# The scatters' stage of a graph layer kernel without TensorE: rows made by VectorE in one step, a predicated copy for crossing rows, no lag between groups

## The reference

```python
x = layernorm(x + L0(x, edge_attr, edge_index))        # attention per destination, 8 heads
# L1:
h = x @ W
e = leaky_relu((h @ a1)[src] + (h @ a2)[dst], 0.2)
attention = softmax(e)                                 # one softmax over all 25000 edges
msgs = attention[:, None] * h[src]
x = layernorm(x + segment_sum(msgs, dst, num_segments=50000))
```

## Time and profile before

| what | value |
|---|---|
| time, median of 3 runs | 1059.08 us (1057.36 to 1061.64) |
| the profiled execution's own time | 1056.71 us |
| its span in the profile | 1055.0 us |
| granted TensorE clock, mean | 0.84 |
| busy over the span: PE, DVE, ACT, POOL | 662.7, 807.1, 705.4, 761.1 us |
| first scatter, last scatter | 790.49, 1046.08 us |
| scatters of this stage | 196 + 1, 195.1 + 1.0 us busy |

### The profile page before, as it was taken

The page is one execution under the profiler, slowest core; times in us unless marked ns, Lnnn a source line. Parts: engine busy times, 40 slices in busy tenths (PEclk is TensorE's granted clock), DMA queues, the critical chain, the costliest instruction groups (busy, mean ns, idle before and its releaser), DMA issues.

```text
span 1055.0 us, 14618 instructions
## 1 busy us (share of the span) xinstructions
PE 662.7 (63%) x3270; PEld 448.6 (43%) x3270; DVE 807.1 (77%) x3723; ACT 705.4 (67%) x2036; POOL 761.1 (72%) x801
## 2 busy tenths in 40 slices
PE   0467777777787677787655656656566555556640
PEld 0246555555565555565444545545432111111110
DVE  4789999999988798896876666666548777777760
ACT  3659998999899797997423444534447666666650
POOL 6777777777777777777077777777737777777775
PEclk9979998999889898988868787878858788778775
DMA  7666786787767678657348777887743322332310
GB/s 200 197 190 200 222 278 210 237 264 231 226 220 238 213 222 258 202 194 226 122 140 285 254 255 248 277 271 248 222 132 93 96 85 86 88 94 85 88 43 25
DMA packets 82013, 196.90 MB, mean 187 GB/s; under 512 B 19814, under 2 KB 22005, under 8 KB 81916
## 3 DMA queue, kind: packets, MB, share of 16 engines
q1 hardware_dynamic: 56774, 148.35, 43.3%
q0 software_dynamic: 25152, 47.63, 16.0%
HBM read 122.71 MB, written 77.22 MB: 190 GB/s over the span
## 4 chain that ended last, share of the span: by engine, by line
POOL 42%; issue 19%; DVE 15%; DMA 8%; ACT 8%; PE 7%; DVEq 1%; SPq 0%; POOLq 0%; ACTq 0%
POOL xs L484 24%; POOL h_res L484 16%; ACT xsT L888 5%; DMA xs<-x_all,row_tab 4%; DVE nst L1408 4%; DVE node_out L1390 4%; POOL out_dram L488 2%; DMA h_res<-in_x,dst_tab 2%; DVE match L1041 1%; DVE part L1395 1%; DVE nmv L1416 1%; ACT logs L898 1%; PE psum L674 1%; PE psum L680 1%; PE psum L597 1%
## 5 line engine op out<-in xcount | busy, mean ns | idle before, releaser
L484 POOL DMA_INDIRECT xs<-x_all,row_tab x196 | 187.7, 958 | 86.9 <-issue 83.0
L488 POOL DMA_INDIRECT out_dram<-yb,at_last x196 | 195.1, 995 | 76.1 <-issue 54.2
L484 POOL DMA_INDIRECT xs<-in_x,src_tab x196 | 187.0, 954 | 61.7 <-issue 58.8
L484 POOL DMA_INDIRECT h_res<-in_x,dst_tab x196 | 187.3, 956 | 59.7 <-issue 59.7
L725 ACT ACTIVATE h_res<-node_in,shift,rstd 128x128 f32<-128x128 f32 (+1 forms) x392 | 155.7, 484 | 0.3 <-DVE shift L1168 0.3
L700 PE MATMUL psum<-node_out,ident_inv 128*128 128x512 f32 x98 | 73.1, 836 | 97.5 <-DVE node_out L1390 97.5
L866 ACT ACTIVATE xsT<-psum 128x512 f32<-128x512 f32 x48 | 28.7, 597 | 145.5 <-PE psum L680 145.2
L1390 DVE SCALAR_TENSOR_TENSOR node_out<-node_out,same_prev,xsT 128x128 f32<-128x128 f32 x196 | 68.6, 350 | 48.5 <-ACT xsT L888 36.2
L725 ACT ACTIVATE yb<-psum,shift,rstd 128x128 f32<-128x128 f32 x196 | 73.6, 455 | 29.2 <-DVE shift L1401 26.5
L552 PE MATMUL psum<-h_res 128*128 128x512 f32 x98 | 59.3, 690 | 41.9 <-ACT h_res L732 41.8
L680 PE MATMUL psum<-ident,xs 128*128 128x128 f32 x192 | 39.8, 344 | 72.7 <-DMA xs<-x_all,row_tab 72.6
(11 more groups left out here) (279 smaller groups left out, 1806.9 us busy)
## 6 DMA issues: line engine op xcount, KB each, us to landing
x1d_in<-x_all SPq DMA_DIRECT2D x98, 256.0 KB, 3.9
node_in<-in_x SPq DMA_DIRECT2D x48, 512.0 KB, 4.3
x_all<-h_res SPq DMA_DIRECT2D x48, 512.0 KB
out_dram<-node_out SPq DMA_DIRECT2D x48, 512.0 KB, 3.3
x_all<-yb SPq DMA_DIRECT2D x49, 256.0 KB, 2.6
src_b<-src_t SPq DMA_DIRECT2D x49, 256.0 KB, 7.3
node_in<-x_all SPq DMA_DIRECT2D x24, 512.0 KB, 5.8
h_res<-in_edge_attr SPq DMA_DIRECT2D x7, 784.0 KB
```

The lines of the kernel that those rows point to most:

```text
L484: return pool.indirect_dma_start(out=to, out_offset=None, in_=table, in_offset=bass.IndirectOffsetOnAxis(ap=idx, axis=0))
L488: return pool.indirect_dma_start(out=table, out_offset=bass.IndirectOffsetOnAxis(ap=idx, axis=0), in_=rows, in_offset=None, bounds_check=l ...
```

## The change

TensorE takes no part in the stage's rows any more. VectorE makes a group's rows in one scalar_tensor_tensor over 512 elements, y = agg x part_scale + x1d_in, written to the PSUM bank (`rows(g)`). A crossing row is kept by one copy_predicated over 512 elements with a mask that is row_tab, now a copy of first_last as int32; `part` is four tiles wide, in the space of dots, and is folded to one tile by two additions at the end. Every group runs in the order running, rows, moments, aggregates, kept, with no lag. Group 0 is done in two halves of two tiles each, its rows in yb instead of PSUM. ScalarE weighs group s + 2 after it has written group s. The transposes and products of the last group's h, which stood between the rows on TensorE, now stand ahead of the loop. Some semaphores that nobody waits for are gone.

```diff
-            for g in range(GROUPS):
-                b = bank[g % 4]
-                pe.wait_ge(x1d_back[g % XI], use(g, XI) * 16)
-                mm(b, ident[:, :], x1d_in[:, g % XI, :], start=True, stop=False)
-                pe.wait_ge(r_chain, (g + 1) * G)
-                mm(b, ident_inv[:, :], agg[:, g % 2, :], start=False, stop=True).then_inc(e_y, 1)
...
             def weigh(g, tiles=range(G)):
+                wait(act, r_chain, (g - 1) * G)
...
-                if s > 0 and edge(s + 2):
-                    weigh(s + 2)
                 act.wait_ge(e_shift, s + 1)
                 if s >= YB:
                     act.wait_ge(e_scat[s % YB], use(s - YB, YB) * 16 * G)
...
+                scale_rows(yb[:, s % YB, :], bank[s % 4], P, range(G), rstd[:, s % 2, :], shift[:, s % 2, :])\
+                    .then_inc(e_applied, 1)
+                if edge(s + 2):
+                    weigh(s + 2)
...
-            def kept(g, t):
-                wait(dve, own_chain, g * G + t)
-                v.scalar_tensor_tensor(part[:, :], tile(agg[:, g % 2, :], t), first_last[:, g * G + t:g * G + t + 1],
-                                       part[:, :], ALU.mult, ALU.add).then_inc(own_chain, 1)
+            ends_here = row_tab
+
+            def kept(g):
+
+                dve.wait_ge(r_chain, (g + 1) * G)
+                wait(dve, own_chain, g)
+                v.copy_predicated(part, ends_here[:, g * G:(g + 1) * G].unsqueeze(2).to_broadcast([P, G, D]),
+                                  agg[:, g % 2, :].rearrange("p (t d) -> p t d", t=G)).then_inc(own_chain, 1)
+
+            def rows(g):
+                dve.wait_ge(x1d_back[g % XI], use(g, XI) * 16)
+                wait(dve, e_applied, g - 3)
+                dve.wait_ge(r_chain, (g + 1) * G)
+                v.scalar_tensor_tensor(bank[g % 4], agg[:, g % 2, :], part_scale[:, :], x1d_in[:, g % XI, :],
+                                       ALU.mult, ALU.add).then_inc(e_y, 1)
...
+            for t in halves[0]:
+                running(0, t)
+            dve.wait_ge(sum_b, 1)
+            c.link(v.reciprocal(inv_sum[:, :], bank[6][:, P:P + 1]))
+            c.link(v.tensor_tensor(part_scale[:, :], fall_p[:, :], inv_sum[:, :], ALU.mult))
+            dve.wait_ge(x1d_back[0], 16)
+            dve.wait_ge(r_chain, 2)
+            first_rows(halves[0])
+            dve.wait_ge(first_y, 1)
+            first_moments(halves[0], first_var)
+            for t in halves[1]:
+                running(0, t)
+            dve.wait_ge(first_rstd, 1)
+            first_shifts(halves[0]).then_inc(first_shift, 1)
+            dve.wait_ge(r_chain, G)
+            first_rows(halves[1])
+            dve.wait_ge(first_y, 2)
+            first_moments(halves[1], e_var)
+            v.memset(part, 0.0)
+            v.tensor_copy(ends_here[:, :], first_last[:, :])
+            c.link(v.tensor_scalar(ident_inv[:, :], ident[:, :], part_scale[:, :], None, ALU.mult))
+            dve.wait_ge(e_rstd, 1)
+            first_shifts(halves[1]).then_inc(e_shift, 1)
+            v.tensor_copy(chunkrow[:, :], bank[6][:, 0:P])
+            kept(0)
+            for g in range(1, GROUPS):
+                if g > 1:
+                    wait(dve, e_y, g - 2)
+                    dve.wait_ge(own_chain, g - 1)
+                running(g, 0)
+                running(g, 1)
+                if g > 1:
+                    shift_of(g - 1)
+                running(g, 2)
+                running(g, 3)
+                rows(g)
+                moments(g)
+                aggregates(g)
+                kept(g)
```

More of the change, by code:

```diff
@@ L885, in weigh @@
             def weigh(g, tiles=range(G)):
+                wait(act, r_chain, (g - 1) * G)
                 for t in tiles:
                     i = g * G + t
-                    fn(tile(xa[:, g % 2, :], t), h_res[:, i * DH:i * DH + D], ACT.Copy, scale=att[:, i:i + 1])\
-                        .then_inc(xa_done, 1)
+                    last = fn(tile(xa[:, g % 2, :], t), h_res[:, i * DH:i * DH + D], ACT.Copy, scale=att[:, i:i + 1])
+                    if g == 0 or t == G - 1:
+                        last.then_inc(xa_done, 1)
             weigh(0, range(0, 2))
@@ L1417, in aggregates, with first_rows @@
                 last.then_inc(e_var, 1)
-            def sums_free(s):
-                if s > 1:
-                    dve.wait_ge(e_y, s - 1)
-                    dve.wait_ge(own_chain, (s - 1) * G)
-            for g in range(HEAD + 1):
-                sums_free(g)
+            def first_rows(tiles):
+                for t in tiles:
+                    last = v.scalar_tensor_tensor(tile(yb[:, 0, :], t), tile(agg[:, 0, :], t), part_scale[:, :],
+                                                  tile(x1d_in[:, 0, :], t), ALU.mult, ALU.add)
+                last.then_inc(first_y, 1)
@@ new lines, in first_moments, with first_shifts @@
+            def first_moments(tiles, done):
+                for t in tiles:
+                    last = v.bn_stats(nst[:, t, :], tile(yb[:, 0, :], t))
+                c.link(last)
+                for t in tiles:
+                    last = v.bn_aggr(nmv[:, 0, t, :], nst[:, t, :])
+                last.then_inc(done, 1)
+            def first_shifts(tiles):
+                return v.scalar_tensor_tensor(shift[:, 0, tiles.start:tiles.stop], nmv[:, 0, tiles.start:tiles.stop, 0], -1.0,
+                                              rstd[:, 0, tiles.start:tiles.stop], ALU.mult, ALU.mult)
@@ L1436, in _ @@
                 running(g, 3)
-                if g == 0:
-                    v.tensor_tensor(part_scale[:, :], fall_p[:, :], inv_sum[:, :], ALU.mult)
-                    v.tensor_copy(chunkrow[:, :], bank[6][:, 0:P])
-                for t in range(G):
-                    kept(g, t)
-                if g < HEAD:
-                    moments(g)
-                    aggregates(g)
-            for s in range(HEAD + 1, GROUPS + 2):
-                if edge(s):
-                    sums_free(s)
-                    running(s, 0)
-                if s - 2 >= HEAD:
-                    shift_of(s - 2)
-                if edge(s):
-                    for t in range(1, G):
-                        running(s, t)
-                if edge(s - 1):
-                    moments(s - 1)
-                if edge(s):
-                    kept(s, 0)
-                if edge(s - 1):
-                    aggregates(s - 1)
-                if edge(s):
-                    for t in range(1, G):
-                        kept(s, t)
+                rows(g)
+                moments(g)
+                aggregates(g)
+                kept(g)
+            shift_of(END)
+            dve.wait_ge(own_chain, GROUPS)
+            c.link(v.tensor_tensor(part[:, 0:2, :], part[:, 0:2, :], part[:, 2:4, :], ALU.add))
+            c.link(v.tensor_tensor(part[:, 0, :], part[:, 0, :], part[:, 1, :], ALU.add))
             dve.wait_ge(f_pe, 1)
```

99 lines of the change are left out of this document (53 added, 46 removed).

## The result

The changed kernel takes 1069.95 us (median of 4 runs, 1068.0 to 1072.54) where before takes 1059.8 (4 runs, 1057.36 to 1061.64): ratio 1.0113, 95% interval 1.0086 to 1.014. It is slower by 10.2 us. The profiled execution's span is 1066.3 us.

A forecast was written before the change was run, and what follows sets the result against it. The prediction took GpSimd's scatter pace, 1.287 us each, to bound the last stage. Group 1's 0.55 us plus about 14 of stops less 2.5 made 12, so 1059.1 + 12 = 1071 us, range 1059.5 to 1084.

The forecast's parts named there:

- What bounds: Last stage: GpSimd's scatters at 1.287 us each set the pace, 247.1 us for 192 steps, something else 2.5.
- Start: Group 0 without TensorE's path: first scatter at 787.44, 3.05 us earlier.
- Group 1: VectorE has more ahead of group 1, so its first scatter comes 0.55 us later than before.
- VectorE's steps: VectorE's period a group: 4.4 us, with predicated copy 0.69 and rows' step 0.75, under GpSimd's 5.15.
- Stops: Scatters wait at their index read for VectorE instructions with two SBUF inputs; about 14 us, less 2.5.
- random formula: With no fixed phase, a VectorE instruction of length d costs (d - 0.14)^2 / 2.574; 15.9 us over 48 groups.
- The age of 0.14 us: A VectorE instruction stops a scatter only if at least 0.14 us old at the scatter's index read.
- The scaling by before: The formula gives 0.14 a group for before, where 0.05 was measured; by that scale stops could cost only 5.8.
- Phase: ScalarE meets its four-buffer limit after 12 to 16 groups; reads then fall 0.18 us into the keep, 17 us if hit.
- The page's inference: Steps with two SBUF inputs do not stall descriptor generation, so wide steps would be free for scatters: 1059.6.
- Sum: 0.55 + about 14 - 2.5 = 12 us on the median of 1059.1, giving 1071.
- the prediction's rule: GpSimd reads indices 0.13 us into an indirect DMA and waits there for VectorE instructions with two SBUF inputs.

The follow-up runs named there:

- e11: e4 with group 1 brought forward by moving VectorE's small preparations; 1053.41 us (12 runs) where before takes 1057.63, ratio 0.9962.
- e2: The changed kernel with a rows' step that reads only one SBUF tensor, the destination's row left out of groups 1 to 48; 1060.01 us in one run.
- e12: The changed kernel with two more BN_AGGR ahead of the predicated copy, which starts 0.13 us later; 1060.98 us in one run.
- e7: e4 with a useless 512-wide TENSOR_TENSOR behind each predicated copy, both inputs in SBUF; 1290.82 us, in a set with standstills.
- e8: e4 with the same useless instruction as e7, but its second input in PSUM; 1300.14 us, in a set with standstills.
- e1: The changed kernel without its predicated copies, the crossing rows' sums left out of the output; 1063.78 us in one profiled run.
- e4: The changed kernel with the running sums agg moved from SBUF to PSUM; 1056.97 us (10 runs) where before takes 1058.96, ratio 0.9987.
- e5: The same kernel as e11, in an earlier set of runs with standstills; 1291.01 us, ratio to before 0.9979.
- e10: The same kernel as e12, in an earlier set of runs with standstills; 1277.4 us where before takes 1299.66.

## Why the prediction was right

- **What bounds.** Right. With the stops gone, e11's stage is GpSimd's pace and its two gaps at the start, to within 0.1 us.
- **Start.** The first scatter was forecast 3.05 us earlier and came 3.09 earlier against the reciprocal (4.03 for 7.12), and it was itself stopped for 0.48 us, which cost nothing, as GpSimd then waited 4.02 us for group 1 anyway.
- **Group 1.** Forecast 0.55 us later, measured 0.32 (13.40 for 13.08). The early start bought nothing, since VectorE's work for group 1 had grown as listed.
- **VectorE's steps.** The predicated copy, which no row showed, was taken at 0.69 and took 0.696; the rows' step 0.75 and 0.759. Two groups next to each other near the start (787.94 us on) run at 4.4 us, as summed: the rows' step began at 788.43 and at 792.84. (The sum adds 0.15 us where the text speaks of 0.1 of waiting; it is 4.3 or 4.4.)
- **Stops.** The mechanism was right, and the size in part by luck. Forecast about 14 us, less the 2.5 that before has; measured 16.7 less 2.5 by the means, 14.2 for 11.5, so the term was 2.7 us too small. The random formula's 15.9 comes nearer only because its parts' errors cancel: it gives 5.6 us for the copies, 6.9 for the rows' steps and 3.3 for the running steps, and measured were 8.7, 6.1 and 1.3, and 0.5 in the first scatter, which was not foreseen.
- **The age of 0.14 us.** The rows of the prediction only put it between 0.09 and 0.18. For wide steps it holds nearly: e2 has a stop at 0.12 and none up to 0.11. For 128-wide steps it is too low: in the changed kernel the read point lay 43 times in a running step that was at least 0.14 us old, and 16 of these scatters were stopped, the youngest at 0.2. That, beside the phase, is why before lies under the formula: there the point lay on such a narrow step 38 times, where an even spread would give some 60 (my estimate, 384 steps x 0.21 / 1.287), and 29 of these were stopped. The scaling by before, 5.8, was wrong, since it carried this over to the wide steps.
- **Phase.** The lock came: ScalarE waits for landings 38 times, from group 11 on (12 to 16 forecast). In it the read lay 0.145 us behind the copy's start instead of 0.18, and the stop of 0.51 us came in every second group, not in each. What the prediction did not have is the other pattern ahead of it, from group 2 to 10, where it took the stops to be random: there the rows' step stopped one scatter in every 4.44 us. e12 suggests, in one run, that 0.13 us decides whether the later pattern has stops.
- **The page's inference** (The Trainium skill, "SBUF — State Buffer", section "Who interferes with whom"), by which steps with two SBUF inputs should leave descriptor generation alone, fails here for indirect DMAs: 1015 against 985 ns in e7 and e8 for the input's place alone. The page's rule that such a step contends with GpSimd's reads agrees.
- **Sum.** 1071 forecast, 1069.95 measured. The medians moved by 10.2 us and the stage by 13.8; the 12 forecast lies between, so the hit on the median is better than the terms were, and that is luck. Whether the 3.6 us between the two is more than the spread of the earlier stages stays open; the runs with the same code there had the reciprocal over a range of 6.8 us.

## What to carry to other kernels

When GpSimd's indirect DMAs set the pace, look at what VectorE has in hand 0.13 us after each of them starts: one 512-wide instruction of 0.7 us with both inputs in SBUF cost up to 0.54 us here. Replacing four narrow steps by a wide one can make that worse even where it saves VectorE time: the four keeps (1.43 us a group) stood behind 1.7 us of stops in before, the copy in their place (0.69 us) behind 8.7. Moving one of the inputs to PSUM changed VectorE's lengths by at most 6 ns and removed the stops. And an early first item is worth nothing if the second is not brought forward with it.

## What was unexpected

- Instructions with a single SBUF input can stop GpSimd too, so the prediction's rule is too narrow. In before's gathers, seven were longer by 0.09 to 0.26 us and ended late with a TENSOR_SCALAR of 512 elements that reads and writes SBUF, always by what was left of it; those at whose read point it was younger than 0.22 us were free. e2's TENSOR_SCALAR, which writes to PSUM, stopped none of six.

```profile
627.25 0.48 DVE L1032 TENSOR_SCALAR reach<-src_b,thr 128x512 bf16<-128x512 f32 x1
627.34 1.20 POOL L484 DMA_INDIRECT xs<-x_all,row_tab  x1 [0.30 <-issue]
```

- In the changed kernel the first scatter (784.86) took 1.47 us; over its read lay a MEMSET of 512 elements (784.84 to 785.32) and then the CAST of the mask to 785.45. It took 1.47 in e1 to e4 as well, and 1.02 in e11, where both were moved away. Which of the two is needed was not tried.
- The stops have a memory. ScalarE waits for landings and VectorE for ScalarE, so they are pulled into step with GpSimd, and stops then repeat or stay away for dozens of groups. e12 gives VectorE 0.13 us more work a group, and its stage is 10.9 us shorter.
- In two sets of runs, on two chips, every kernel took 20% or more longer (before: 1302.15 and 1299.66 us, 23%). The profiles of e5 to e10 show gaps of up to 5.6 us between scatters about every 26 us, during part of which VectorE and ScalarE stood as well. It is no lasting property of a chip: on the second of them before took 1057.63 us in a later set. The profiles name no cause, and I have none.
- TensorE's granted clock in the stage was 0.50 throughout, that is 1.2 GHz, with 4.3 us of work in 285, where before it was 0.80, 0.75 and 0.68 in three stretches. e11, with the same 0.50, is faster than before, so the clock is not what made the changed kernel slower.
